# 128-wide attention of a two-layer decoder: another order of scores, transposes and the fourth quarter

## The chip, the cores and the metric

One core of a Trainium2 chip runs the whole program. The metric is the device time in microseconds. A core has engines that run their own instruction lists in order: TensorE (PE in the profile; its weight loads are PEld), VectorE (DVE), ScalarE (ACT), GpSimd (POOL) and the DMA queues of SyncE (SP). They wait for one another by semaphores: a waiting instruction holds up everything behind it on its engine.

## The reference, cut to what matters

The program is a decoder of two layers over `x`, 16 sequences of 64 tokens, 256 wide: attention and cross attention, a mixture of experts, causal attention, then the stage that is changed (a cross attention with 16 heads of width 128), and a second mixture of experts. The changed stage computes, for each sequence `b`:

```python
h  = layernorm(x[b])                                  # 64 x 256
kv = concatenate([ctx[b], h])                         # 128 keys x 256
q  = rope(rms_norm(h @ Wq.T))                         # 16 heads x 64 x 128
k  = rope(rms_norm(kv @ Wk.T))                        # 4 heads x 128 keys x 128
v  = kv @ Wv.T                                        # 4 heads x 128 keys x 128
p  = softmax(q @ k.T / sqrt(128))                     # 4 query heads share a k and a v
x[b] = x[b] + concatenate_heads(p @ v) @ Wo.T
```

## The kernel before, in words

`attention128` works through NT = 8 tiles of 128 tokens, two sequences each. A tile needs:

- `turn_h`: PE transposes the normed input (made by DVE's `norm_a`, POOL's `root` and DVE's `norm_b`); ACT's `h_out` and DVE's `low` split it into two f16 parts.
- `fill(n, u, k)`, k = 0 to 7: six f16 matmuls each (L896), 512 columns of queries (k 0 to 3) or of keys and values of one sequence (4 and 6 keys, 5 and 7 values), into PSUM banks `xpr0` and `xpr1` in turn. A fill waits until the bank's reader is done.
- Each of the six fills of queries and keys is squared by ACT (`square`, L788); then DVE's `rope` sums the squares and makes three products with the tables (L1065 to L1069), and POOL adds the halves (`add`, L733). After the fourth and the sixth `rope`, DVE's `mean_square` and POOL's `rms_root` (L738) make the factors that DVE's `scale` (L1083) applies. Fills 5 and 7 are copied by ACT (`v_copy`).
- `turn_qk(n, i)`: PE transposes a scaled block (L943) into `xpt0` or `xpt1`, ACT copies it out (`qk_out`); i 0 to 3 are queries, 4 and 5 keys ("K4", "K5").
- Four quarters of the attention, each with four heads: `scores` (L905, into `xps0` or `xps1` in turn), DVE's `maxes` (a maximum, L1088, and a small product, L1090), ACT's `exps` (four exponentials, L798), DVE's `normalise` (reciprocal L1095, product L1097), PE's `turn_probs` (L913), ACT's `pt_copy`, PE's `pv` (product with V, L925), ACT's `o_copy` (L808).
- `project`: PE multiplies by Wo in four steps of four matmuls (L933), DVE's `residual` adds to x (L1101).

The tiles are skewed. `skewed` runs `early(0)`, then `mixed(n, n+1)` for n = 0 to 6, and `late(7)`. A `mixed` period does the attention of tile n, the fills, rope and scale of tile n+1, the transposed input of tile n+2, and the projection of tile n-1. Within a period each engine's order is written out by hand, once for each engine; no scheduler changes it. A period begins here, for the reader's counting, with PE's `fill(n+1, 0)`.

The banks `xpt0` and `xpt1` are taken in turn by all transposes of a period, so each transpose has a running number j: it waits until transpose j-2 is copied out, and its reader waits for number j+1. `T_K`, `T_P`, `T_Q`, `T_H` hold these numbers. Eleven transposes are made in a period.

Of the kernel before, what the change touches and what calls it, by code (L numbers as in the profile page):

```python
# [20 lines left out]
NT = B * S // P  # L21
DC = D // P
H = 16
# [642 lines left out]
def attention128(nc, C, w):  # L666
# [5 lines left out]
    with m.stack:  # L672
# [34 lines left out]
        FIRST_T, STEP_T = 6, 11  # L707
        T_K, T_P, T_Q, T_H = (0, 1), (2, 3, 4, 6), (5, 7, 8, 10), 9

        def turns(n, u):  # L710

            base = n * STEP_T + FIRST_T
            if type(n) is int and n == NT - 1:
                base -= 1
                return base, lambda k: (base + k) % 2
            return base, lambda k: (u + k) % 2

        def t_q(n, i):
            return T_Q[i] - (i == 3 and not there(n + 2))
# [42 lines left out]
        def _(act):  # L762
# [15 lines left out]
            def qk_out(j, i, bank):  # L778
# [32 lines left out]
            def early(n, u):  # L811
                h_out(0, 0, 0, 0)
                for k in (0, 1, 2, 3, 4):
                    square(0, k)
                    if k == 1:
                        h_out(1, 1, 1, 1)
                v_copy(0, 0, 5)
                square(0, 6)
                v_copy(0, 0, 7)
                act.wait_ge(t_out, 2)  # L820
                for i in range(4):
                    qk_out(2 + i, i, i % 2)

            def mixed(n, u, n1, u1):
                base, bank = turns(n, u)
                square(n1, 0)
                qk_out(base + T_K[0], 4, bank(T_K[0]))
                square(n1, 1)
                qk_out(base + T_K[1], 5, bank(T_K[1]))
# [12 lines left out]
                exps(n, 3)  # L842
                pt_copy(n, 2, base + T_P[2], bank(T_P[2]))
                qk_out(base + T_Q[0], 0, bank(T_Q[0]))
                v_copy(n1, u1, 7)
                pt_copy(n, 3, base + T_P[3], bank(T_P[3]))
                qk_out(base + T_Q[1], 1, bank(T_Q[1]))
                o_copy(n, u, 2)
                qk_out(base + T_Q[2], 2, bank(T_Q[2]))
                if there(n + 2):  # L850
                    h_out(n + 2, u, base + T_H, bank(T_H))
                o_copy(n, u, 3)
                if there(n + 2):
                    act.wait_ge(t_out, base + T_H + 1)
                qk_out(base + t_q(n, 3), 3, bank(t_q(n, 3)))

            def late(n, u):
                base, bank = turns(n, u)
                qk_out(base, 4, bank(0))
                qk_out(base + 1, 5, bank(1))  # L860
                exps(n, 0)
                exps(n, 1)
                pt_copy(n, 0, base + 2, bank(2))
                pt_copy(n, 1, base + 3, bank(3))
                o_copy(n, u, 0)
                exps(n, 2)
                o_copy(n, u, 1)
                exps(n, 3)
                pt_copy(n, 2, base + 4, bank(4))
                pt_copy(n, 3, base + 5, bank(5))  # L870
                o_copy(n, u, 2)
                o_copy(n, u, 3)
# [4 lines left out]
        def _(pe):  # L877
# [82 lines left out]
            def mixed(n, u, n1, u1):  # L960
                base, bank = turns(n, u)

                def project_before(quarter):
                    if there(n - 1):
                        project(n - 1, 1 - u, quarter)
# [3 lines left out]
                turn_qk(n, 4, base + T_K[0], bank(T_K[0]))  # L969
                project_before(0)  # L970
                fill(n1, u1, 1)
                turn_qk(n, 5, base + T_K[1], bank(T_K[1]))
                project_before(1)
                pe.wait_ge(t_out, base + 2)
# [15 lines left out]
                fill(n1, u1, 6)  # L990
                turn_probs(n, 2, base + T_P[2], bank(T_P[2]))
                turn_qk(n1, 0, base + T_Q[0], bank(T_Q[0]))
                fill(n1, u1, 7)
                turn_probs(n, 3, base + T_P[3], bank(T_P[3]))
                turn_qk(n1, 1, base + T_Q[1], bank(T_Q[1]))
                pv(n, u, 2, base + T_P[2])
                turn_qk(n1, 2, base + T_Q[2], bank(T_Q[2]))
                if there(n + 2):
                    pe.wait_ge(t_out, base + T_H - 1)
                    turn_h(n + 2, u, base + T_H, bank(T_H))  # L1000
                pv(n, u, 3, base + T_P[3])
                turn_qk(n1, 3, base + t_q(n, 3), bank(t_q(n, 3)))

            def late(n, u):
                base, bank = turns(n, u)
                turn_qk(n, 4, base, bank(0))
                turn_qk(n, 5, base + 1, bank(1))
                for quarter in range(4):
                    project(n - 1, 1 - u, quarter)
                pe.wait_ge(t_out, base + 2)  # L1010
                scores(n, 0)
                scores(n, 1)
                turn_probs(n, 0, base + 2, bank(2))
                turn_probs(n, 1, base + 3, bank(3))
                pv(n, u, 0, base + 2)
                scores(n, 2)
                pv(n, u, 1, base + 3)
                scores(n, 3)
                turn_probs(n, 2, base + 4, bank(4))
                turn_probs(n, 3, base + 5, bank(5))  # L1020
                pv(n, u, 2, base + 4)
                pv(n, u, 3, base + 5)
# [6 lines left out]
        def _(dve):  # L1029
# [92 lines left out]
            def mixed(n, u, n1, u1):  # L1122
# [19 lines left out]
                mean_square(n1, 1)  # L1142
                normalise(n, 3)
# [5 lines left out]
                if there(n + 2):  # L1149
                    low(n + 2, u, turns(n, u)[1](T_H))  # L1150

            def late(n, u):
                maxes(n, 0)
                maxes(n, 1)
                residual(n - 1, 1 - u)
                normalise(n, 0)
                normalise(n, 1)
                maxes(n, 2)
# [1061 lines left out]
```

## Time and profile before

| | |
|---|---|
| median of 3 runs | 1053.54 us (1050.61 to 1055.73) |
| profiled execution | 1049.7 us, its span 1047.9 us |
| busy over the span | PE 829.2, DVE 673.1, ACT 486.8, POOL 321.5 us |
| changed stage | from about 453 us to 745 us of the span |
| starts of PE's fill 0 of the periods n = 0 to 6 | 481.90, 513.47, 546.58, 579.66, 612.75, 645.75, 678.70 us |
| last tile's projection starts, its residual ends | 737.49, 745.12 us |

Times are microseconds from the start of the span. In a timeline row stand the start, the length, the engine, the line, the operation, what it writes and reads, its shape, how many were merged, and in brackets how long the engine was idle before it and who ended that idle time.

### The profile page before, as it was taken

Reading aid. Unit: us, or ns where it says so; the run is one execution under the profiler, and the core shown is the slowest. Engines: PE = TensorE matmul, PEld = TensorE weight load, DVE = VectorE, ACT = ScalarE, POOL = GpSimd, SP = SyncE. Lnnn points to the kernel's source line nnn. Section 1 sums busy time; section 2 is a strip of 40 time slices with the busy share of each in tenths; the row PEclk is TensorE's granted clock in tenths of the full one; section 3 lists DMA queues with packets and bytes.
Section 4 is the critical chain, followed back from the end, with each engine's and each line's share of the span. In section 5 each row is a group of like instructions: output and inputs, shape, how many; then the busy total and the mean of one; then the engine's idle time right before and its main releaser. Section 6 shows DMA issues by size and latency. Waiting matters only on the chain. (4 is left out here: it accounts for less than half of the span.)

```text
span 1047.9 us, 16118 instructions
## 1 busy us (share of the span) xinstructions
PE 829.2 (79%) x5470; PEld 545.3 (52%) x5470; DVE 673.1 (64%) x1381; ACT 486.8 (46%) x1235; POOL 321.5 (31%) x281
## 2 busy tenths in 40 slices
PE   3899762347997078767888988897649999999997
PEld 2677642216875066623666766666524444444443
DVE  3778964635764279557788777883346565656654
ACT  1765431115566046514565555654244544454453
POOL 1113763660000554324445424440021221211210
PEclk9999975578999599869999999999659999999999
DMA  9900003227985211000000000000115443444431
GB/s 311 419 29 2 2 2 131 72 80 221 329 301 180 60 48 55 1 1 1 1 1 1 0 0 1 1 1 1 48 50 142 122 123 105 130 115 113 132 91 41
DMA packets 35398, 90.71 MB, mean 87 GB/s; under 512 B 6406, under 2 KB 8969, under 8 KB 34826
## 3 DMA queue, kind: packets, MB, share of 16 engines
q1 hardware_dynamic: 32266, 81.63, 24.4%
q0 software_dynamic: 3072, 8.30, 2.5%
q8 instruction: 35, 0.57, 0.2%
q14 instruction: 25, 0.20, 0.1%
HBM read 67.71 MB, written 22.29 MB: 86 GB/s over the span
## 5 line engine op out<-in xcount | busy, mean ns | idle before, releaser
L1199 POOL TENSOR_TENSOR m1ws<-m1raw,m1ws 128x768 f16<-128x768 f32 x33 | 55.0, 1669 | 219.0 <-ACT m1raw L1202 219.0
L733 POOL TENSOR_TENSOR xqr<-xqr,xt 128x512 f32<-128x512 f32 x48 | 61.2, 1276 | 140.7 <-DVE xt L1069 140.7
L1509 DVE TENSOR_TENSOR m1sg<-m1sg,m1Wb 128x512 f32<-128x512 f32 x66 | 61.1, 926 | 64.0 <-ACT m1sg L1427 53.1
L1469 PE MATMUL m1pg<-m1hs,m1ws 128*128 128x512 f16 x396 | 97.5, 383 | 3.8 <-PEq L58 3.8
L1480 PE MATMUL m1py<-m1ap,m1ws 128*128 128x512 f16 x396 | 96.3, 379 | 1.6 <-DVE m1ap L1521 1.6
L1469 PE MATMUL m1pu<-m1hs,m1ws 128*128 128x512 f16 x396 | 97.0, 381 | 0.0
L1431 ACT ACTIVATE m1ap<-m1ac 128x512 f16<-128x512 f32 x66 | 41.6, 630 | 116.1 <-DVE m1ac L1515 116.1
L1521 DVE TENSOR_TENSOR m1ap<-m1ac,m1ap 128x512 f16<-128x512 f32 x66 | 45.7, 693 | 45.9 <-ACT m1ap L1431 45.9
L1565 POOL DMA_INDIRECT rows<-slots_out,slot x32 | 32.7, 1022 | 116.5 <-DMA slots_out<-m0yo 103.4
L1469 PEld LDWEIGHTS m1pg<-m1hs,m1ws 128*128 128x128 f16 x396 | 38.9, 98 | 51.3 <-issue 5.3
L1480 PEld LDWEIGHTS m1py<-m1ap,m1ws 128*128 128x128 f16 x396 | 38.6, 98 | 48.8 <-DVE m1ap L1521 2.6
L788 ACT ACTIVATE xsq<-xpr 128x512 f32<-128x512 f32 x48 | 28.8, 601 | 75.3 <-PE xpr L896 75.3
L1469 PEld LDWEIGHTS m1pu<-m1hs,m1ws 128*128 128x128 f16 x396 | 39.0, 98 | 47.6 <-issue 1.6
L933 PE MATMUL xpo<-xwo,xOT 128*128 128x256 f32 x256 | 59.6, 380 | 0.7 <-ACT xOT L808 0.7
L798 ACT ACTIVATE xE<-xps,xnb 128x128 f32<-128x128 f32 x128 | 45.5, 379 | 23.5 <-DVE xnb L1090 23.5
L896 PE MATMUL xpr<-xparts,xhs 128*128 128x512 f16 x192 | 49.4, 397 | 8.1 <-DVE xkv L1049 5.2
L1065 DVE TENSOR_REDUCE xss<-xsq 128x4 f32<-128x512 f32 x48 | 32.7, 682 | 35.1 <-ACT xsq L788 34.6
L933 PEld LDWEIGHTS xpo<-xwo,xOT 128*128 128x128 f32 x256 | 47.1, 190 | 7.4 <-ACT xOT L808 1.3
L896 PE MATMUL xpr<-xparts,xkv 128*128 128x512 f16 x192 | 47.6, 387 | 3.4 <-DVE xt L1069 3.4
L1990 PE MATMUL m0ph<-m0xs,m0wg 128*128 128x256 f16 x384 | 48.2, 276 | 2.2 <-DVE m0xs L2026 2.0
L1427 ACT ACTIVATE m1sg<-m1pg 128x512 f32<-128x512 f32 x66 | 39.4, 596 | 18.2 <-PE m1pg L1469 18.2
L1515 DVE SCALAR_TENSOR_TENSOR m1ac<-m1pu,m1sg 128x512 f32<-128x512 f32 x66 | 45.6, 691 | 2.5
(289 smaller groups left out, 1921.5 us busy)
## 6 DMA issues: line engine op xcount, KB each, us to landing
m1Wb<-wt_dram SPq DMA_DIRECT2D x66, 256.0 KB, 4.0
m1raw<-in_m_w SPq DMA_DIRECT2D x33, 384.0 KB, 4.2
slots_in<-zeros SPq DMA_DIRECT2D x1, 8192.0 KB, 26.6
m0rg<-in_m_wgu SPq DMA_DIRECT2D x16, 512.0 KB, 6.9
m0xg<-slots_in SPq DMA_DIRECT2D x32, 256.0 KB, 4.6
slots_out<-m0yo SPq DMA_DIRECT2D x32, 256.0 KB, 3.6
m0rd<-in_m_wd SPq DMA_DIRECT2D x8, 512.0 KB, 7.6
xwo<-in_x_wo SPq DMA_DIRECT2D x1, 2048.0 KB, 17.8
```

The lines of the kernel that those rows point to most:

```text
L733: pool.tensor_tensor(blk, blk, t2[:, k % 2, :, :], ALU.add).then_inc(add_ok, 1)
L798: ins = act.activation(E[:, c, :], p_s[k % 2][:, i, :], ACT.Exp, bias=nb[:, c:c + 1], scale=XSCALE, accum_out=sm[:, c:c + 1])
L896: ins = pe.matmul(p_r[k % 2][:, :, :].rearrange("p h d -> p (h d)"), lhs, rhs, start=(i == 0), stop=(i == 5))
L933: ins = pe.matmul(p_o[u][:, 0:D], OT[:, h, :, :].rearrange("p b q -> p (b q)"), wo[:, h, :], start=(h == 0), stop=(h == XH - 1))
L1199: pool.tensor_tensor(ws[:, u, 1, :], raw[:, u, :], ws[:, u, 0, :], ALU.subtract).then_inc(prep_ok, 1)
L1431: act.activation(ap[:, q, 0, :], ac[:, q, :], ACT.Copy).then_inc(ah_ok, 1)
L1469: ins = pe.matmul(bank[:, :], part(ws, u, sw, c, which), hs[:, sh, c, CH * q:CH * q + CH], start=(k == 0), stop=(k == 5))
L1480: ins = pe.matmul(p_y[c][q][:, :], ws[:, u, sw, GU + P * c:GU + P * c + P], ap[:, q, sa, :], start=(first and k == 0), stop=(last and k == ...
L1509: dve.tensor_tensor(sg[:, q, :], sg[:, q, :], Wb[:, u, CH * q:CH * q + CH], ALU.mult).then_inc(sw_ok, 1)
L1515: dve.scalar_tensor_tensor(ac[:, q, :], p_u[q][:, :], 1.0 / (H_UP * W_UP), sg[:, q, :], ALU.mult, ALU.mult).then_inc(act_ok, 1)
L1521: dve.tensor_tensor(ap[:, q, 1, :], ac[:, q, :], ap[:, q, 0, :], ALU.subtract).then_inc(al_ok, 1)
L1990: ins = pe.matmul(p_h[u][:, which, :], wg[:, u, sw, P * (2 * c + which):P * (2 * c + which) + P], xs[:, u, sx, c, :], start=(i == 0), stop ...
```

## The change

Three things are done in the order of the work; no operation is added or removed, and every shape stays.

1. Scores: PE makes the third quarter's scores right behind fill 4 and the fourth's right behind fill 5, ahead of the transposes and the products with V. DVE takes the third quarter's maxima ahead of `normalise(n, 1)`, the fourth's right behind the fifth `rope`. ACT makes the third quarter's exponentials ahead of the first `pt_copy`, and the fourth's ahead of the second. The two products with V of quarters 1 and 2 stand together, ahead of fill 6.
2. The fourth quarter: `normalise(n, 3)` is DVE's last work of the period. Its transposes, `pt_copy`, product with V and `o_copy` go into the next period, behind its fill 1 ("before" in `ORDER`).
3. The projection of tile n-1 is done in two steps of eight matmuls, before and behind fill 3, instead of four steps of four.

The numbers of the transposes now come from the tuple `ORDER`. `late` is changed in the same manner.

```diff
-        FIRST_T, STEP_T = 6, 11
-        T_K, T_P, T_Q, T_H = (0, 1), (2, 3, 4, 6), (5, 7, 8, 10), 9
+        ORDER = ("K4", "before", "K5", "P0", "P1", "P2", "Q0", "Q1", "Q2", "H", "Q3")
...
 # ScalarE, mixed
+                if there(n - 1):
+                    pt_copy(n - 1, 3, *turn("before"))
+                qk_out(5, *turn("K5"))
+                if there(n - 1):
+                    o_copy(n - 1, 1 - u, 3)
...
                 square(n1, 4)
-                pt_copy(n, 0, base + T_P[0], bank(T_P[0]))
+                exps(n, 2)
+                pt_copy(n, 0, *turn("P0"))
                 v_copy(n1, u1, 5)
-                pt_copy(n, 1, base + T_P[1], bank(T_P[1]))
+                exps(n, 3)
+                pt_copy(n, 1, *turn("P1"))
                 o_copy(n, u, 0)
-                exps(n, 2)
                 o_copy(n, u, 1)
                 square(n1, 6)
-                exps(n, 3)
...
 # TensorE, mixed
                 fill(n1, u1, 1)
+                if there(n - 1):
+                    turn_probs(n - 1, 3, *turn("before"))
+                turn_qk(n, 5, *turn("K5"))
+                if there(n - 1):
+                    pv(n - 1, 1 - u, 3, turn("before")[0])
+                pe.wait_ge(t_out, turn("K5")[0] + 1)
                 scores(n, 0)
                 fill(n1, u1, 2)
                 scores(n, 1)
-                project_before(2)
+                project_before(0, 1)
                 fill(n1, u1, 3)
-                project_before(3)
+                project_before(2, 3)
                 pe.wait_ge(ctx_ok, n1 + 1)
                 fill(n1, u1, 4)
-                turn_probs(n, 0, base + T_P[0], bank(T_P[0]))
+                scores(n, 2)
+                turn_probs(n, 0, *turn("P0"))
                 fill(n1, u1, 5)
-                turn_probs(n, 1, base + T_P[1], bank(T_P[1]))
-                pv(n, u, 0, base + T_P[0])
-                scores(n, 2)
-                pv(n, u, 1, base + T_P[1])
                 scores(n, 3)
+                turn_probs(n, 1, *turn("P1"))
+                pv(n, u, 0, turn("P0")[0])
+                pv(n, u, 1, turn("P1")[0])
                 fill(n1, u1, 6)
...
 # VectorE, mixed
                 rope(n1, 3)
                 mean_square(n1, 0)
+                maxes(n, 2)
                 normalise(n, 1)
                 if there(n - 1):
                     residual(n - 1, 1 - u)
                 rope(n1, 4)
+                maxes(n, 3)
+                normalise(n, 2)
                 if there(n + 2):
                     norm_a(n + 2, u)
-                maxes(n, 2)
                 scale(n1, 0)
-                maxes(n, 3)
-                normalise(n, 2)
                 rope(n1, 5)
                 mean_square(n1, 1)
-                normalise(n, 3)
                 scale(n1, 1)
...
                 if there(n + 2):
-                    low(n + 2, u, turns(n, u)[1](T_H))
+                    low(n + 2, u, turns(n, u)[1]("H")[1])
+                normalise(n, 3)
...
 # TensorE, late
                 turn_qk(n, 4, *turn("K4"))
+                turn_probs(n - 1, 3, *turn("before"))
                 turn_qk(n, 5, *turn("K5"))
+                pv(n - 1, 1 - u, 3, turn("before")[0])
+                pe.wait_ge(t_out, turn("K5")[0] + 1)
+                scores(n, 0)
+                scores(n, 1)
                 for quarter in range(4):
                     project(n - 1, 1 - u, quarter)
```

PE in the period n = 5, from fill 3 to fill 6. `xpr` is the target of a fill, `xpo<-xwo` the projection, `xpt<-ident,xE` the transposed probabilities, `xps` scores, `xpo<-xPT` a product with V. Before:

```order
L896 MATMUL xpr<-xparts,xhs 128x512 x6
L933 MATMUL xpo<-xwo,xOT 128x256 x4
L896 MATMUL xpr<-xparts,xkv 128x512 x6
L913 MATMUL xpt<-ident,xE 128x128 x4
L896 MATMUL xpr<-xparts,xkv 128x512 x6
L913 MATMUL xpt<-ident,xE 128x128 x4
L925 MATMUL xpo<-xPT,xV 128x256 x2
L905 MATMUL xps<-xKT,xQT 128x128 x4
L925 MATMUL xpo<-xPT,xV 128x256 x2
L905 MATMUL xps<-xKT,xQT 128x128 x4
L896 MATMUL xpr<-xparts,xkv 128x512 x6
```

The same place in the changed kernel:

```order
L899 MATMUL xpr<-xparts,xhs 128x512 x6
L936 MATMUL xpo<-xwo,xOT 128x256 x8
L899 MATMUL xpr<-xparts,xkv 128x512 x6
L908 MATMUL xps<-xKT,xQT 128x128 x4
L916 MATMUL xpt<-ident,xE 128x128 x4
L899 MATMUL xpr<-xparts,xkv 128x512 x6
L908 MATMUL xps<-xKT,xQT 128x128 x4
L916 MATMUL xpt<-ident,xE 128x128 x4
L928 MATMUL xpo<-xPT,xV 128x256 x4
L899 MATMUL xpr<-xparts,xkv 128x512 x6
```

Each group of scores now stands ahead of a group of transposes, and both products with V (x4) stand together between the second transposes and fill 6.

DVE in the period n = 5, from the fourth `mean_square` factor to the next `rope`. `xsv` is the mean square, `xE` the normalised probabilities, `x` the residual, `xss` and `xqr` the beginning of a rope, `xmx` and `xnb` a quarter's maxima. Before:

```order
L1076 TENSOR_SCALAR xsv<-xss 128x16
L1095 RECIPROCAL xrc<-xsm 128x4
L1097 TENSOR_TENSOR xE<-xE,xrc 128x512
L1101 TENSOR_TENSOR x<-x,xpo 128x256
L1065 TENSOR_REDUCE xss<-xsq 128x4
L1066 TENSOR_TENSOR xqr<-xpr,xraw 128x512
L1069 TENSOR_TENSOR xt<-xpr,xraw 128x4x64 x2
L1034 BN_STATS xst<-x 128x6
```

The same place in the changed kernel:

```order
L1082 TENSOR_SCALAR xsv<-xss 128x16
L1094 TENSOR_REDUCE xmx<-xps 128x4
L1096 TENSOR_SCALAR xnb<-xmx 128x4
L1101 RECIPROCAL xrc<-xsm 128x4
L1103 TENSOR_TENSOR xE<-xE,xrc 128x512
L1107 TENSOR_TENSOR x<-x,xpo 128x256
L1071 TENSOR_REDUCE xss<-xsq 128x4
L1072 TENSOR_TENSOR xqr<-xpr,xraw 128x512
L1075 TENSOR_TENSOR xt<-xpr,xraw 128x4x64 x2
L1094 TENSOR_REDUCE xmx<-xps 128x4
L1096 TENSOR_SCALAR xnb<-xmx 128x4
```

The third quarter's maxima have come in ahead of the second quarter's normalisation, the residual and the fifth rope; the fourth quarter's follow that rope.

ACT in the same period, between two of its squares (`xsq`). `xPT` is a `pt_copy`, `xV` a `v_copy`, `xOT` an `o_copy`, `xE,xsm` a quarter's four exponentials. Before:

```order
L788 ACTIVATE xsq<-xpr 128x512
L765 ACTIVATE xPT<-xpt 128x512
L792 ACTIVATE xV<-xpr 128x512
L765 ACTIVATE xPT<-xpt 128x512
L808 ACTIVATE xOT<-xpo 128x8x64
L798 ACTIVATE xE,xsm<-xps,xnb 128x128 x4
L808 ACTIVATE xOT<-xpo 128x8x64
L788 ACTIVATE xsq<-xpr 128x512
```

The same place in the changed kernel:

```order
L788 ACTIVATE xsq<-xpr 128x512
L798 ACTIVATE xE,xsm<-xps,xnb 128x128 x4
L765 ACTIVATE xPT<-xpt 128x512
L792 ACTIVATE xV<-xpr 128x512
L798 ACTIVATE xE,xsm<-xps,xnb 128x128 x4
L765 ACTIVATE xPT<-xpt 128x512
L808 ACTIVATE xOT<-xpo 128x8x64 x2
L788 ACTIVATE xsq<-xpr 128x512
```

Each of the two copies of transposed probabilities now has a quarter's exponentials ahead of it.

## Rows read from the trace of the kernel before

**Rows 1.** Busy time by stretch: periods 0, 2 and 6; us, then each engine's busy us.

```profile
481.90:513.47 31.57, 24.81 (x140) 15.82 (x138) 27.51 (x56) 18.82 (x58) 13.97 (x9) 0.97 0.00 1
...
546.58:579.66 33.08, 29.81 (x171) 21.68 (x171) 26.86 (x57) 18.70 (x58) 13.97 (x9) 1.00 0.00 1
...
678.70:711.68 32.98, 30.02 (x173) 21.93 (x173) 25.51 (x50) 18.56 (x56) 12.93 (x8) 1.00 0.00 1
```

**Rows 2.** Timeline of PE in period 2 (starts at 546.58).

```profile
546.58 1.47 PE L896 MATMUL xpr<-xparts,xhs 128*128 128x512 f16 x6 [0.64 <-DVE xkv L1049]
...
547.88 0.60 PE L943 MATMUL xpt<-ident,xqr 128*128 128x128 f32 x4
...
548.32 1.89 PE L933 MATMUL xpo<-xwo,xOT 128*128 128x256 f32 x8
...
550.05 1.46 PE L896 MATMUL xpr<-xparts,xhs 128*128 128x512 f16 x6
...
565.81 1.05 PE L905 MATMUL xps<-xKT,xQT 128*128 128x128 f32 x8
...
566.70 1.03 PE L925 MATMUL xpo<-xPT,xV 128*128 128x256 f32 x4
...
570.96 0.66 PE L913 MATMUL xpt<-ident,xE 128*128 128x128 f32 x4 [1.04 <-DVE xE L1097]
...
574.94 0.65 PE L913 MATMUL xpt<-ident,xE 128*128 128x128 f32 x4 [1.59 <-DVE xE L1097]
...
577.34 0.38 PE L881 MATMUL xpt<-ident,xhn 128*128 128x128 f32 x2
```

**Rows 3.** Timeline of DVE, ACT and POOL in period 2.

```profile
545.69 0.42 DVE L1048 SCALAR_TENSOR_TENSOR xhs<-xpt,xhs 128x256 f16<-128x256 f32 x1 [0.63 <-ACT xkv L775]
...
548.08 0.60 ACT L788 ACTIVATE xsq<-xpr 128x512 f32<-128x512 f32 x1 [0.93 <-PE xpr L896]
...
556.53 0.69 DVE L1065 TENSOR_REDUCE xss<-xsq 128x4 f32<-128x512 f32 x1 [1.03 <-ACT xsq L788]
...
558.39 0.68 DVE L1088 TENSOR_REDUCE xmx<-xps 128x4 f32<-128x512 f32 x1
...
558.55 1.26 POOL L733 TENSOR_TENSOR xqr<-xqr,xt 128x512 f32<-128x512 f32 x1 [3.08 <-DVE xt L1069]
...
559.10 0.73 DVE L1090 TENSOR_SCALAR xnb<-xmx 128x4 f32<-128x4 f32 x1
...
559.75 0.17 DVE L1095 RECIPROCAL xrc<-xsm 128x4 f32<-128x4 f32 x1
...
560.56 0.68 DVE L1065 TENSOR_REDUCE xss<-xsq 128x4 f32<-128x512 f32 x1
...
562.69 1.70 DVE L1097 TENSOR_TENSOR xE<-xE,xrc 128x512 f32<-128x512 f32 x1
...
564.32 0.41 DVE L1101 TENSOR_TENSOR x<-x,xpo 128x256 f32 x1
...
568.46 0.37 ACT L798 ACTIVATE xE<-xps,xnb 128x128 f32<-128x128 f32 x1 [1.85 <-DVE xnb L1090]
...
569.85 0.61 ACT L808 ACTIVATE xOT<-xpo 128x512 f32<-128x512 f32 x1
```

**Rows 4.** Timeline of DVE and POOL at the end of the first tile's ropes.

```profile
477.17 3.56 DVE L1083 TENSOR_TENSOR xqr<-xqr,xsr 128x512 f32<-128x512 f32 x4
...
477.26 1.71 POOL L733 TENSOR_TENSOR xqr<-xqr,xt 128x512 f32<-128x512 f32 x1 [1.74 <-DVE xt L1069]
...
481.07 1.29 DVE L1083 TENSOR_TENSOR xqr<-xqr,xsr 128x512 f32<-128x512 f32 x2 [0.34 <-POOL xsr L738]
```

**Rows 5.** Timeline of PE in the last tile.

```profile
733.31 3.49 PE L925 MATMUL xpo<-xPT,xV 128*128 128x256 f32 x8
...
737.49 7.17 PE L933 MATMUL xpo<-xwo,xOT 128*128 128x256 f32 x32 [0.69 <-ACT xOT L808]
```

**Rows 6.** Stretch of the last tile: us, PE busy us, granted clock, DMA.

```profile
734.00:736.00 2.00, 2.00 (x6) 0.50 0.00 0
```

More of the change, by code:

```diff
@@ L703, in attention128, with turn @@
                  " scaled t_ok t_out s_ok max_ok nb_ok exp_ok rc_ok e_ok o_ok o_out proj_ok x_ok high_ok chigh_ok")
-        FIRST_T, STEP_T = 6, 11
-        T_K, T_P, T_Q, T_H = (0, 1), (2, 3, 4, 6), (5, 7, 8, 10), 9
+        ORDER = ("K4", "before", "K5", "P0", "P1", "P2", "Q0", "Q1", "Q2", "H", "Q3")
         def turns(n, u):
-            base = n * STEP_T + FIRST_T
+            order = [k for k in ORDER if k not in (() if there(n - 1) else ("before",)) + (() if there(n + 2) else ("H",))]
             if type(n) is int and n == NT - 1:
[L714 to L719, printed above, removed]
+                order = order[:6] + ["P3"]
+            base = n * len(ORDER) + (6 if type(n) is int and n == 0 else 4 if type(n) is int and n == NT - 1 else 5)
+            def turn(what):
+                k = order.index(what)
+                return base + k, (base + k if type(n) is int else u + 1 + k) % 2
+            return base, turn
         block = m.stack.enter_context(nc.Block())
@@ L852, in mixed @@
[L852 to L855, printed above, removed]
-            def late(n, u):
-                base, bank = turns(n, u)
-                qk_out(base, 4, bank(0))
-                qk_out(base + 1, 5, bank(1))
+                    h_out(n + 2, u, *turn("H"))
+                    act.wait_ge(t_out, turn("H")[0] + 1)
+                qk_out(3, *turn("Q3"))
+            def late(n, u):
+                _, turn = turns(n, u)
+                qk_out(4, *turn("K4"))
+                pt_copy(n - 1, 3, *turn("before"))
+                qk_out(5, *turn("K5"))
+                o_copy(n - 1, 1 - u, 3)
@@ L960, in mixed, with project_before @@
             def mixed(n, u, n1, u1):
[L961 to L965, printed above, removed]
+                base, turn = turns(n, u)
+                def project_before(*quarters):
+                    for quarter in quarters:
+                        if there(n - 1):
+                            project(n - 1, 1 - u, quarter)
                 pe.wait_ge(t_out, base - 1)
                 fill(n1, u1, 0)
-                turn_qk(n, 4, base + T_K[0], bank(T_K[0]))
-                project_before(0)
+                turn_qk(n, 4, *turn("K4"))
                 fill(n1, u1, 1)
-                turn_qk(n, 5, base + T_K[1], bank(T_K[1]))
-                project_before(1)
-                pe.wait_ge(t_out, base + 2)
+                if there(n - 1):
+                    turn_probs(n - 1, 3, *turn("before"))
+                turn_qk(n, 5, *turn("K5"))
+                if there(n - 1):
+                    pv(n - 1, 1 - u, 3, turn("before")[0])
+                pe.wait_ge(t_out, turn("K5")[0] + 1)
                 scores(n, 0)
@@ L993, in mixed @@
                 fill(n1, u1, 7)
[L994 to L997, printed above, removed]
+                turn_qk(n1, 1, *turn("Q1"))
+                pv(n, u, 2, turn("P2")[0])
+                turn_qk(n1, 2, *turn("Q2"))
                 if there(n + 2):
-                    pe.wait_ge(t_out, base + T_H - 1)
-                    turn_h(n + 2, u, base + T_H, bank(T_H))
@@ L1001, in mixed @@
-                pv(n, u, 3, base + T_P[3])
-                turn_qk(n1, 3, base + t_q(n, 3), bank(t_q(n, 3)))
+                    pe.wait_ge(t_out, turn("H")[0] - 1)
+                    turn_h(n + 2, u, *turn("H"))
+                turn_qk(n1, 3, *turn("Q3"))
             def late(n, u):
-                base, bank = turns(n, u)
-                turn_qk(n, 4, base, bank(0))
-                turn_qk(n, 5, base + 1, bank(1))
+                _, turn = turns(n, u)
+                turn_qk(n, 4, *turn("K4"))
@@ L1014, in late @@
[L1014 to L1015 removed]
                 scores(n, 2)
[L1017 removed]
+                turn_probs(n, 0, *turn("P0"))
                 scores(n, 3)
[L1019 to L1022, printed above, removed]
+                turn_probs(n, 1, *turn("P1"))
+                pv(n, u, 0, turn("P0")[0])
@@ L1023, in late @@
+                turn_probs(n, 2, *turn("P2"))
+                pv(n, u, 1, turn("P1")[0])
+                turn_probs(n, 3, *turn("P3"))
+                pv(n, u, 2, turn("P2")[0])
+                pv(n, u, 3, turn("P3")[0])
                 for quarter in range(4):
```

44 lines of the change are left out of this document (19 added, 25 removed).

## The prediction, as it was put on record

> **What bounds the kernel now.** I read four things in order. First the stretches by period: a steady period takes 33.08 us, PE is busy 29.81 of it, DVE 26.86, ACT 18.70, at a granted clock of 1.00 (the full level, 2.4 GHz) [rows 1]. So PE comes nearest to a bound, and the question is what it waits for in the other 3.3 us. Then PE's timeline: it waits 1.04 us ahead of the third quarter's transposes and 1.59 us ahead of the fourth's, each time for DVE's normalisation, and 0.64 us ahead of the next fill 0, for DVE's low part [rows 2]. The change aims at the first two. Third, the timelines of DVE and ACT, for the length of each step and for what delays it: a product of 128x4 takes 0.73 us at 559.10, because it ends when POOL's addition of 558.55 ends (559.81); a normalisation that falls on such an addition takes 1.70 us [rows 3]. Last, the beginning and the end of the stage, where a scale right behind a rope and a low clock can be seen [rows 4 to 6].
>
> **Price list**, from starts of neighbours. PE: fill 547.88-546.58 = 1.30 to the next instruction, turned block 548.32-547.88 = 0.44, a half of four projection matmuls 550.05-548.32 = 1.73, scores 566.70-565.81 = 0.89, a product with V the same less a little, 0.87 (busy 1.03 against 1.05) [rows 2]. A fill's square starts 548.08-546.58 = 1.50 after the fill and takes 0.60, as any 128x512 copy of ACT does; exponentials 569.85-568.46 = 1.39; rope 558.39-556.53 = 1.86 to the next DVE instruction; normalisation without POOL in the way 560.56-559.75 = 0.81; maxima directly behind a rope 559.10+0.73-558.39 = 1.44, since POOL's addition always starts then; without it 0.90 (0.68, 0.17 and a gap; estimate) [rows 3]. Handing over to another engine costs some 0.04 (fill 0 ends at 548.05, its square starts at 548.08).
>
> **The change, part by part.** Nothing is added or removed, and no DMA is in it, so what counts is one period, walked from its fill 0 (time 0) to the next.
>
> *Start of the period.* Fill 0 at 0, K4 1.30, fill 1 1.74, the fourth quarter's transposes 3.04 (normalised at about 1.0, in the idle time that DVE has ahead of the first rope, so that edit costs DVE nothing), K5 3.48. The product with V must wait for ACT: square 1 at 3.24 to 3.84, then the copy to 4.44, so it starts at 4.45, an idle time of 0.53. Scores 1 at 5.3, fill 2 6.2, scores 2 7.5, eight projection matmuls 8.4, fill 3 11.9, eight more 13.2, fill 4 16.6, third scores 17.9, done at 18.97. The two halves of the projection in one are free.
>
> *The new wait on DVE.* The fourth rope starts at 14.0 as before (560.56-546.58 = 13.98 [rows 3]) and ends at 15.9. Next stand the third maxima, which need the scores of 18.97. Behind them are queued normalisation 1, the residual and the fifth rope. DVE so idles 3.1 us, and goes on: maxima 19.0 to 19.9, normalisation 20.7, residual 21.0 (564.32 to the next rope is 0.33, estimate from its 0.41 busy), fifth rope 21.0 to 22.9. Before, the residual stood at 564.32-546.58 = 17.7 and the rope at 18.1 [rows 3]: 2.9 us late. Normalisation 1 gets out of POOL's way (1.70 to 0.69), which is in these numbers.
>
> *The new wait on PE.* Fourth maxima 22.9 to 24.35 (POOL's fifth addition is in the way), fourth exponentials on ACT 24.4 to 25.75, and only behind these the copy of quarter 2's transposed probabilities, to 26.35. PE's second product with V needs that copy. PE had come to it at 17.92+0.89+0.44+1.30+0.89+0.44+0.87 = 22.8, or 23.1 with the first copy behind the third exponentials. So PE stands still for 3.3 us, with fills 6 and 7 and three blocks behind it. This is the dear one. Then product 26.4, fill 6 27.3 (before: 21.9, one scores' 0.89 behind 567.57 = 566.70+0.87), its square 28.8 to 29.4, sixth rope 29.4 to 31.3.
>
> *The end of the period.* The wait for normalisation 3 is gone, but block Q1 needs scale 1, which needs the sixth rope: Q1 at 31.3+0.07+0.75 = 32.1. Behind a rope the early tile shows what follows: the scale goes first and POOL's addition is stretched to 1.71, and scale 4 starts 481.07-477.17 = 3.90 after the first scale, the last two take 1.29 [rows 4]. So the last scale ends at 31.3+0.07+3.90+1.29 = 36.5, the low part follows, and the next fill 0 starts 546.58-545.69 = 0.89 after the low part's start [rows 2, 3], at 37.35. The way over the transposed input is shorter: with Q2 at 34.2 behind the delayed third scale, `turn_h` at 34.6 and 579.66-577.34 = 2.32 more [rows 2] make 37.0.
>
> A steady period is thus 37.3 against 33.08: **+4.3**. Bounds: with no POOL in the way of the fourth maxima 0.55 less; and if the low part does not wait for the last scale 0.35 less, so +3.3 at least; upward, the first scale at the contended 1.70 instead of 0.70 adds up to 1.0, so +5.3 at most. I take the middle, because rows 3 and 4 show just these neighbours.
>
> The Trainium skill says in "SBUF — State Buffer", section "Who interferes with whom", that a VectorE instruction with two SBUF inputs and a GpSimd one that reads SBUF shut each other out for the whole instruction, whoever starts first. The 1.70 against 0.69 agrees. By it alone a scale just behind the rope could also lose the port; that is the upper bound.
>
> *Sum.* Period 0 (31.57 now [rows 1]) has no tile before it, so no projection stands ahead of its fill 4 and DVE hardly waits for the third scores; only the stop ahead of the second product with V remains, and the same walk gives +1.9. Periods 1 to 5: 5 x 4.26 = 21.3. Period 6 and the last tile together: the sixth rope again at +29.4; K4 after scale 4; normalisation 3 is no longer hidden, its transposes come at 37.5, scores at 39.7; the projection of tile 6 (16 matmuls, 6.9 us) now covers the first two quarters' exponentials; the remaining chain of maxima, exponentials and copies ends with the last copy at 58.0. Before, that was 737.49-678.70 = 58.8, in which the two last products took 3.49 instead of 1.74 at a granted clock of 0.50 [rows 5, 6]. So -0.8. Together +22.4 us.
>
> **The clock.** In the last tile, after a stretch in which PE stopped again and again for normalisations, the granted clock fell to 0.50 (the 1.2 GHz level), and the low stretch cost 3.49-1.74 = 1.75 us [rows 5, 6]. In the changed kernel each period has a complete stop of 3.3 us, longer than any in a steady period now, and some 2 us at its end. If the clock falls after the first, fill 6 on the chain runs slow; what it can cost is between 0 and 1.75, I take 1.1, for six periods: +6.6, or 7 with some at the end. The Trainium skill, "TensorE: Matmul & The Clock Gate", section "HAM oscillation — how this bites in real kernels", tells of the same thing, a loop whose every burst starts cold behind a wait. It speaks against this change; by the rows alone the fall is likely, not sure.
>
> So the profiled execution of 1049.7 would become 1049.7+22.4+7 = 1079; the median of the runs, 3.8 above that execution, becomes 1053.5+29 = **1082 us**.
>
> **The rivals.**
>
> - *Waits as walked, clock stays up.* 1053.5+22.4 = 1076. For it: a gap on PE alone did not always bring the clock down (at 1.00 in all steady periods, with waits of 1.59). Chance 0.27; forecast with the clock 0.50.
> - *The clock falls twice in most periods*, at the stop and again at the period's end, so that fill 0 to scores start slow: 2 x 1.75 x 6 = 21 on top of 22.4, at most 1097. 0.11.
> - *The other side: the removed waits decide.* If the order on ACT let the copy pass in time, the period would be PE's work plus the way over `turn_h`: fill 0 to `turn_h` 28.8, and 2.32, so 31.1, 1.95 less than now, over six periods 12 us: 1042. It decides if the fourth maxima were ready before 19.6 or so. Against it: these wait for the fifth rope, which waits for fill 4 at 16.6. 0.07.
> - *The moved waits cancel*: the stop on PE takes 1.0 us instead of 3.3, because DVE's order costs less than read. Then each period is as before. 0.05, 1053.
>
> Half a per cent, 5.3 us, is what measuring can tell from no change. Slower by more: 0.50+0.27+0.11 = 0.88; within: 0.05; faster: 0.07. The range from 1066 to 1095 leaves out about two in ten: the other side, the cancelled case, and the far end of the twice fallen clock. Its lower end is +3.3 a period for five periods less 4 for the ends of the stage (1053.5+12.5), its upper end the clock cost near its maximum in most periods.
>
> **What would show it.** In the trace of the changed kernel: starts of fill 0 about 37 to 39 us apart; PE idle about 3 us ahead of the product with V behind the second transposes, released by ACT's copy; DVE idle about 3 us ahead of the third maxima, released by scores; no wait of PE for the third or fourth normalisation; granted clock under 1.00 in the steady periods; the last tile shorter by about 5 us from its K4. I am wrong if the period is under 34 us, if the stop on PE is under 1.5 us, or if the fifth rope starts before the third maxima.

## The result, and the profile after

The changed kernel takes 1087.96 us in the median of 4 runs (1083.94 to 1089.87), the kernel before 1054.63 us in 4 runs (the three told above and one more of 1057.54). The ratio is 1.0319, 95% interval 1.0292 to 1.0346. The profiled execution took 1087.24 us with a span of 1085.4 us, 37.5 more than the span before. That is more than the 33.3 between the medians, because the profiled execution of the kernel before (1049.7 us) was shorter than any of its four runs.

The busy times by stretch, with the columns of [rows 1], of periods 0, 2, 4 and 6:

```profile
482.19:515.42 33.23, 24.22 (x131) 15.33 (x130) 25.66 (x54) 17.88 (x56) 13.49 (x9) 0.94 0.00 0
...
554.67:593.32 38.65, 32.18 (x171) 22.50 (x171) 26.25 (x57) 18.87 (x58) 13.60 (x9) 0.96 0.00 1
...
632.56:673.35 40.79, 35.20 (x170) 24.28 (x171) 26.21 (x57) 19.18 (x57) 13.62 (x9) 0.87 0.00 0
...
713.36:751.00 37.64, 32.92 (x168) 23.13 (x168) 23.36 (x49) 18.48 (x55) 12.96 (x8) 0.91 0.00 1
```

A steady period takes 38.65 to 40.79 us (fill 0 of periods 1 to 6 starts at 515.42, 554.67, 593.32, 632.56, 673.35 and 713.36) against 33.08. DVE and ACT are busy for about as long as before; PE's busy time in a steady period has grown from 29.81 to between 32.18 and 35.20 us without one added instruction, and the granted clock is 0.87 to 0.96 in place of 1.00.

PE's timeline of period 2 of the changed kernel, whose fill 0 starts at 554.67 (compare [rows 2]):

```profile
554.67 1.47 PE L899 MATMUL xpr<-xparts,xhs 128*128 128x512 f16 x6 [0.90 <-DVE xkv L1055]
...
559.04 1.13 PE L928 MATMUL xpo<-xPT,xV 128*128 128x256 f32 x4 [0.30 <-ACT xPT L765]
...
572.59 1.05 PE L908 MATMUL xps<-xKT,xQT 128*128 128x128 f32 x8
...
576.75 1.13 PE L928 MATMUL xpo<-xPT,xV 128*128 128x256 f32 x4
...
581.02 1.71 PE L928 MATMUL xpo<-xPT,xV 128*128 128x256 f32 x4 [3.15 <-ACT xPT L765]
...
582.52 2.61 PE L899 MATMUL xpr<-xparts,xkv 128*128 128x512 f16 x6
...
588.54 0.65 PE L946 MATMUL xpt<-ident,xqr 128*128 128x128 f32 x4 [1.25 <-DVE xqr L1089]
```

The waits for normalisations are gone. In their place PE stops for 3.15 us ahead of the second product with V, released by ACT's copy. The six matmuls of the fill behind it then take 2.61 us instead of 1.46. At the end PE waits again, for block Q1 (1.25) and for the low part (0.90).

DVE, ACT and POOL in the same period (compare [rows 3]):

```profile
573.68 0.69 DVE L1094 TENSOR_REDUCE xmx<-xps 128x4 f32<-128x512 f32 x1 [2.98 <-PE xps L908]
...
575.30 0.41 DVE L1107 TENSOR_TENSOR x<-x,xpo 128x256 f32 x1
...
575.63 0.68 DVE L1071 TENSOR_REDUCE xss<-xsq 128x4 f32<-128x512 f32 x1
...
577.48 0.68 DVE L1094 TENSOR_REDUCE xmx<-xps 128x4 f32<-128x512 f32 x1
...
577.64 1.26 POOL L733 TENSOR_TENSOR xqr<-xqr,xt 128x512 f32<-128x512 f32 x1 [2.82 <-DVE xt L1075]
...
578.20 0.73 DVE L1096 TENSOR_SCALAR xnb<-xmx 128x4 f32<-128x4 f32 x1
...
578.96 0.37 ACT L798 ACTIVATE xE<-xps,xnb 128x128 f32<-128x128 f32 x1 [1.86 <-DVE xnb L1096]
...
580.36 0.61 ACT L765 ACTIVATE xPT<-xpt 128x512 f32<-128x512 f32 x1
...
585.80 0.69 DVE L1071 TENSOR_REDUCE xss<-xsq 128x4 f32<-128x512 f32 x1 [4.58 <-ACT xsq L788]
...
587.73 0.69 DVE L1089 TENSOR_TENSOR xqr<-xqr,xsr 128x512 f32<-128x512 f32 x1
...
587.82 1.72 POOL L733 TENSOR_TENSOR xqr<-xqr,xt 128x512 f32<-128x512 f32 x1 [6.18 <-DVE xt L1075]
...
588.33 1.36 DVE L1048 TENSOR_SCALAR xhn<-x,xmv 128x256 f32 x1
```

To be read from top to bottom: DVE waits 2.98 us for the third scores, with normalisation, residual and fifth rope (575.63) behind; the fourth maxima follow that rope, and their small product takes 0.73 us beside POOL's addition; only then come the exponentials (578.96) and the copy (580.36) that lets PE go on. The sixth rope starts at 585.80, 31.1 us after fill 0, after 4.58 us without work for DVE. Behind it POOL's addition is stretched to 1.72 and DVE's norm_b to 1.36.

PE's busy time and granted clock in steps of 2 us over the stop:

```profile
578.00:580.00 2.00, 0.00 (x0) 1.00 0.00 0
...
580.00:582.00 2.00, 0.98 (x3) 0.86 0.00 0
...
582.00:584.00 2.00, 2.00 (x6) 0.50 0.00 0
...
584.00:586.00 2.00, 2.00 (x13) 0.79 0.00 0
```

The clock falls to 0.50 with the stop: in period 2 half a microsecond behind its end, in others up to 1.3 us ahead of it (in period 1 at about 540.5 us, with PE going on at 541.84). It does so in each of the seven periods, and twice more with fill 0, behind the waits at the period's end (632 to 636 and 673 to 677 us). The last tile's products with V and the start of the last projection (compare [rows 5]):

```profile
771.04 1.98 PE L928 MATMUL xpo<-xPT,xV 128*128 128x256 f32 x8
...
773.71 7.17 PE L936 MATMUL xpo<-xwo,xOT 128*128 128x256 f32 x32 [0.69 <-ACT xOT L808]
```

The eight matmuls took 1.98 us, at the full clock, against 3.49 at 0.50 in the kernel before. From the last tile's first transposed block (K4, 751.59 us here, about 710.7 before) to this projection pass 22.1 us instead of 26.8.

### The profile page after: what moved, and what is told of

Read it like the earlier page. It is cut to its first block and busy times, and to the rows that moved or that the text cites. A ratio compares the mean times of both kernels' runs of the same rounds, so it can differ in the third digit from the quotient of the medians.

```text
span 1085.4 us, 16122 instructions
## 1 busy us (share of the span) xinstructions
PE 852.6 (79%) x5470; PEld 557.1 (51%) x5470; DVE 665.0 (61%) x1381; ACT 489.7 (45%) x1235; POOL 319.0 (29%) x281
## 5 line engine op out<-in xcount | busy, mean ns | idle before, releaser
L733 POOL TENSOR_TENSOR xqr<-xqr,xt 128x512 f32<-128x512 f32 x48 | 64.4, 1341 | 175.6 <-DVE xt L1075 175.6
L1571 POOL DMA_INDIRECT rows<-slots_out,slot x32 | 32.7, 1023 | 111.7 <-DMA slots_out<-m0yo 98.7
L928 PE MATMUL xpo<-xPT,xV 128*128 128x256 f32 x128 | 41.2, 452 | 25.0 <-ACT xPT L765 24.8
L899 PE MATMUL xpr<-xparts,xhs 128*128 128x512 f16 x192 | 53.3, 420 | 9.2 <-DVE xkv L1055 6.8
L899 PE MATMUL xpr<-xparts,xkv 128*128 128x512 f16 x192 | 54.4, 427 | 3.3 <-DVE xt L1075 3.3
```

What stands on the lines that cost most here:

```text
L733: pool.tensor_tensor(blk, blk, t2[:, k % 2, :, :], ALU.add).then_inc(add_ok, 1)
L899: ins = pe.matmul(p_r[k % 2][:, :, :].rearrange("p h d -> p (h d)"), lhs, rhs, start=(i == 0), stop=(i == 5))
L928: ins = pe.matmul(p_o[(u + k) % 2][:, 256 * g:256 * g + 256], V[:, u, k // 2, 2 * (k % 2) + g, :], PT[:, k % 2, 2 * g:2 * g + 2, :].rearra ...
```

## The experiments

Eight kernels were run. The change as a whole stands at 1.0319. Each ratio is to the kernel before in the same chip's runs; periods are means over periods 1 to 5 of the one profile of each kernel, from the starts of fill 0; "end" is from fill 0 of period 6 to the last residual's end.

| kernel | ratio, 95% interval | period | end |
|---|---|---|---|
| before | 1 | 33.05 | 66.42 |
| changed | 1.0319, 1.0292 to 1.0346 | 39.59 | 67.98 |
| e1_copy_first | 1.0063, 1.0046 to 1.0081 | 35.15 | 63.62 |
| e2_spare_matmuls | 1.0220, 1.0187 to 1.0252 | 36.96 | 67.00 |
| e3_quarter4_alone | 0.9965, 0.9945 to 0.9986 | 33.25 | 62.04 |
| e4_scores_alone | 1.0316, 1.0278 to 1.0354 | 38.00 | 71.79 |
| e5_square_first | 0.9982, 0.9965 to 1.0000 | 34.30 | 62.38 |
| e6_norm_first | 1.0248, 1.0225 to 1.0271 | 37.58 | 66.30 |
| e7_input_early | 0.9859, 0.9837 to 0.9881 | 31.55 | 63.29 |
| e8_input_early_before | 1.0038, 1.0018 to 1.0058 | 34.01 | 66.43 |

**e1_copy_first**, from the changed kernel, ACT in `mixed`:

```diff
                 v_copy(n1, u1, 5)
-                exps(n, 3)
                 pt_copy(n, 1, *turn("P1"))
+                exps(n, 3)
                 o_copy(n, u, 0)
```

> One pair on ScalarE is exchanged in the mixed periods of the changed kernel: the copy of the second quarter's transposed probabilities stands ahead of the fourth quarter's exponentials. Theory A (the stop ahead of the second product with V comes from this copy being queued behind exponentials that wait for the fifth rope): PE's stop of 3.15 us ahead of that product falls under 0.5 us; but the exponentials now sit ahead of the square of fill 6, so the sixth rope comes only about 1.8 us earlier (27.6 instead of 29.4 after fill 0) and not 3.2. With the clock falling less often, the period goes from 39.6 to 35.5 to 37 us, the kernel from 1088 to about 1066 to 1074. Rival B (the period is set by VectorE's late third maxima and the long end behind the sixth rope, the stop on PE is only slack): the period changes by less than 0.5 us, the kernel stays within 3 us of 1088.

Measured: one exchanged pair takes away 2.6 of the 3.2 per cent. In period 2 (fill 0 at 544.26) the two products with V run without a stop, and the sixth rope starts 27.3 us after fill 0 (31.1 in the changed kernel):

```profile
566.32 2.03 PE L928 MATMUL xpo<-xPT,xV 128*128 128x256 f32 x8
...
571.56 0.69 DVE L1071 TENSOR_REDUCE xss<-xsq 128x4 f32<-128x512 f32 x1 [0.74 <-ACT xsq L788]
```

The period is 34.8 us where the clock stays up and 36.4 in the one period (613.97 to 650.38) in which it fell at fill 0. A ratio of 1.0063 is 1061 us beside the 1054.63 of before, 5 less than the lower end of what was expected. The period is below the 35.5 to 37 expected, and the clock fell in only one of the five. Rival B is out: the stop is no slack.

**e2_spare_matmuls**, from the changed kernel, PE in `mixed`; `spare` waits for the residual and issues twelve f16 matmuls of 128x512 into the bank that the next product overwrites:

```diff
                 pv(n, u, 0, turn("P0")[0])
+                spare(n, u, u1)
                 pv(n, u, 1, turn("P1")[0])
```

> The changed kernel with 12 spare matmuls (128x512, f16, 0.22 us each at the full level, 2.6 us together) on PE ahead of the second product with V, written into the PSUM bank that this product overwrites; they fill the stop of 3.2 us and change no result. Theory A (some 2.2 us of each period's +6.5 are the granted clock that falls after the stop): the clock stays at 1.00 there, the period falls from 39.6 to about 37.5, where the walk over the waits alone puts it, and the kernel from 1088 to about 1075. Rival B (the low clock is only a sign of idleness and costs nothing on the chain of waits): the period stays at 39.6 or grows by what the spare matmuls add, the kernel is 1088 or more.

Measured: with 77 more matmuls in the record (84 were added) the kernel is a per cent faster than the changed one. In period 2 (fill 0 at 545.62) the stop is 0.57 us, since the spare work fills it, but the next product starts no sooner in the chain of waits, 26.35 us after fill 0 as in the changed kernel; the fill behind it takes 1.46 us, and the clock of the whole period is 1.00:

```profile
568.64 2.75 PE L935 MATMUL xpo<-xparts,xhs 128*128 128x512 f16 x12
...
571.97 1.13 PE L928 MATMUL xpo<-xPT,xV 128*128 128x256 f32 x4 [0.57 <-ACT xPT L765]
...
572.94 1.46 PE L899 MATMUL xpr<-xparts,xkv 128*128 128x512 f16 x6
...
545.62:582.58 36.96, 33.08 (x182) 23.05 (x183) 26.27 (x57) 18.80 (x58) 13.60 (x9) 1.00 0.00 1
```

The period is 36.96 at a granted clock of 1.00, against 39.59: the clock costs 2.6 us a period, where 2.2 were expected. Rival B is out.

**e3_quarter4_alone**, from the changed kernel: scores, maxima and exponentials of quarters 3 and 4 back where they were in the `mixed` periods; the last tile keeps the changed order.

```diff
 # TensorE, mixed
                 fill(n1, u1, 4)
-                scores(n, 2)
                 turn_probs(n, 0, *turn("P0"))
                 fill(n1, u1, 5)
-                scores(n, 3)
                 turn_probs(n, 1, *turn("P1"))
                 pv(n, u, 0, turn("P0")[0])
+                scores(n, 2)
                 pv(n, u, 1, turn("P1")[0])
+                scores(n, 3)
 # ScalarE and VectorE: exps(n, 2), exps(n, 3), maxes(n, 2), maxes(n, 3), normalise(n, 2) likewise
```

> One part alone: the fourth quarter's normalisation, transposes and product with V in the next period and the projection in two steps, as in the changed kernel, but scores, maxima and exponentials of quarters 3 and 4 in the order of the kernel before. Theory A (the order of scores and exponentials brings the stop; moving quarter 4 by itself costs little): no stop above 1 us on PE, clock at 1.00, the fifth rope at about 18.7 after fill 0; but 1.3 us of quarter 4's work and 0.5 us of waiting stand ahead of fill 6, so the period is about 34 us against 33.1, the kernel about 1054.6 + 6 x 0.9 - 3 (shorter last tile) = 1057. Rival B (moving quarter 4 is what lengthens the period, since everything behind fill 1 comes later): 1075 or more. Rival C (the two removed waits pay): 1042 to 1048.

Measured: 0.9965, so this part of the change is a small gain. The period is 33.25 us, hardly longer than before, not the 34 expected; the gain comes from the end, 62.04 against 66.42 us, of which about 1.5 us are the low clock in the kernel before's last products with V (3.49 against 1.98 us). PE does what it did in [rows 1] and the clock stays up:

```profile
549.13:582.39 33.26, 30.19 (x171) 21.84 (x171) 26.89 (x57) 18.73 (x58) 13.55 (x9) 1.00 0.00 1
```

**e4_scores_alone**, from the kernel before: the same groups moved forward, quarter 4 and the last tile left alone.

```diff
 # TensorE, mixed (order of the changed kernel)
+                scores(n, 2)
                 turn_probs(n, 0, base + T_P[0], bank(T_P[0]))
                 fill(n1, u1, 5)
+                scores(n, 3)
                 turn_probs(n, 1, base + T_P[1], bank(T_P[1]))
                 pv(n, u, 0, base + T_P[0])
-                scores(n, 2)
                 pv(n, u, 1, base + T_P[1])
-                scores(n, 3)
 # ScalarE and VectorE likewise
```

> The other part alone: the kernel before, with scores, maxima and exponentials of quarters 3 and 4 moved forward as in the changed kernel; quarter 4 stays in its period, the projection in four steps, the last tile as before. Theory A (this order makes the stop): PE stops for about 3.6 us ahead of the second product with V, the clock falls in most periods, the period is 36.2 us from the waits alone and 37.5 to 39 with the clock, the kernel 1054.6 + 6 x 3.1 = 1073 without and 1080 to 1090 with the clock. Rival B (it is the combination with quarter 4 that stops PE): period under 34, the kernel within 5 us of 1055.

Measured: 1.0316, all of the loss. In period 2 (fill 0 at 552.72) stands the same stop:

```profile
577.20 2.07 PE L925 MATMUL xpo<-xPT,xV 128*128 128x256 f32 x4 [3.15 <-ACT xPT L765]
...
579.06 2.10 PE L896 MATMUL xpr<-xparts,xkv 128*128 128x512 f16 x6
```

Its profiled period of 38.0 lies in the expected 37.5 to 39, the ratio in the upper half of what was expected. Rival B is out. The periods are shorter than in the changed kernel (38.0 against 39.59) and the end, with the old last tile, longer (71.79 against 67.98).

One period of this run prices the clock without any spare work. In period 3 (fill 0 at 591.48) the stop is the same, but the clock stays at 1.00:

```profile
615.96 1.13 PE L925 MATMUL xpo<-xPT,xV 128*128 128x256 f32 x4 [3.15 <-ACT xPT L765]
...
591.48:627.73 36.25, 29.96 (x171) 21.80 (x171) 26.25 (x57) 18.90 (x59) 13.55 (x9) 1.00 0.00 0
```

It takes 36.25 us, where 36.2 were expected from the waits alone; the other four take 37.95 to 38.76 (in two of them the clock falls twice). So the waits cost 3.2 us here and the clock 1.7 to 2.5 more, and a stop of 3.15 us does not bring the clock down every time.

**e5_square_first**, from the changed kernel:

```diff
                 v_copy(n1, u1, 5)
-                exps(n, 3)
                 pt_copy(n, 1, *turn("P1"))
                 o_copy(n, u, 0)
                 o_copy(n, u, 1)
                 square(n1, 6)
+                exps(n, 3)
```

> The changed kernel with ScalarE's fourth exponentials put behind the square of fill 6 (behind the copy of quarter 2's probabilities and both output copies too). e1_copy_first took the stop off PE, and its period is 34.8 us; there the square of fill 6 still stands behind the exponentials, which wait for the fourth maxima. Theory A (what sets the period is when the sixth rope starts, and that needs this square): the sixth rope starts some 1.4 us sooner, the period is 33.4 to 33.8 us, the clock stays at 1.00, ratio to the kernel before 0.995 to 1.000. Rival B (after e1 the late fifth rope is the bound): period and ratio as in e1, 34.8 us and 1.006.

Measured: 0.9982. The sixth rope starts 572.50-546.02 = 26.5 us after fill 0, 0.8 sooner than in e1 instead of 1.4, and the period is 33.9 us where the clock stays up (35.7 in the one where it fell), a little over the 33.4 to 33.8 expected. So with ACT's list fitted to it the changed kernel is back at the time of the kernel before. The order of scores is not free by that: e3, which has the rest of the change, has a period of 33.25 us, 0.7 less.

**e6_norm_first**, from the changed kernel, DVE:

```diff
-                maxes(n, 2)
                 normalise(n, 1)
                 if there(n - 1):
                     residual(n - 1, 1 - u)
+                maxes(n, 2)
                 rope(n1, 4)
```

> The changed kernel with VectorE's third maxima behind the second normalisation and the residual instead of ahead of them; all else as in the changed kernel, the stop on PE too. Theory A (VectorE's wait of 3.0 us for the third scores delays the two steps behind it, and by them the fifth rope, the fourth maxima and all that follows): VectorE does these two steps inside the wait, the fifth rope starts about 1.1 us sooner, the period falls by 1.1 us, and the clock falls as before; ratio 1.024 to 1.028 against 1.032. Rival B (that wait is slack): ratio unchanged at 1.03 or more.

Measured: 1.0248 against 1.0319. DVE's wait for the third scores is 0.83 us and the stop on PE 2.12 us, a microsecond less, in period 2 (fill 0 at 555.00):

```profile
574.00 0.69 DVE L1094 TENSOR_REDUCE xmx<-xps 128x4 f32<-128x512 f32 x1 [0.83 <-PE xps L908]
...
580.30 1.91 PE L928 MATMUL xpo<-xPT,xV 128*128 128x256 f32 x4 [2.12 <-ACT xPT L765]
...
582.01 2.40 PE L899 MATMUL xpr<-xparts,xkv 128*128 128x512 f16 x6
```

The mean period is 2.0 us shorter, not 1.1. Period 2, in which the clock falls once in both kernels, is 1.04 shorter (37.61 against 38.65). The clock still falls with the stop (2.40 us for the fill), but at no period's end, and it comes back sooner (in period 1 after 3.4 us at 0.50, in the changed kernel after 6.8). The remainder is put down to that; no run shows it by itself.

**e7_input_early**, from e3_quarter4_alone:

```diff
-        ORDER = (..., "P2", "Q0", "Q1", "Q2", "H", "Q3")
+        ORDER = (..., "P2", "Q0", "H", "Q1", "Q2", "Q3")
 # ScalarE
                 qk_out(0, *turn("Q0"))
+                h_out(n + 2, u, *turn("H"))
                 v_copy(n1, u1, 7)
+                act.wait_ge(t_out, turn("H")[0] + 1)
                 qk_out(1, *turn("Q1"))
 # TensorE: fill 0 waits for base - 3 instead of base - 1, and
                 fill(n1, u1, 7)
+                turn_h(n + 2, u, *turn("H"))
                 turn_qk(n1, 1, *turn("Q1"))
 # VectorE
                 scale(n1, 0)
+                norm_b(n + 2, u)
                 maxes(n, 3)
...
                 scale(n1, 1)
-                norm_b(n + 2, u)
+                low(n + 2, u, ...)
                 scale(n1, 2)
                 scale(n1, 3)
+                low_ctx(n + 2, u)
                 scale(n1, 4)
                 scale(n1, 5)
-                low(n + 2, u, ...)
                 normalise(n, 3)
```

> A version meant to beat both. From e3_quarter4_alone, with one more change: the transposed input of tile n+2 is made earlier. norm_b goes ahead of the fourth maxima, turn_h behind fill 7 and ahead of block Q1, h_out ahead of the copy of values, the low part of it directly behind scale 1, the low part of the context behind scale 3; PE's fill 0 no longer waits for the last block's copies. Theory (in e3 the end of the period, from the sixth rope to the next fill 0, is 7.5 us long because the low part waits for the last scales, which wait for POOL's root): fill 0 starts when PE is through with Q3, about 31.5 us after the last fill 0 instead of 33.25, six times: 10 us less than e3, ratio to the kernel before about 0.986. Rival B (VectorE is the bound by then, with POOL's addition in its way): period 33 us or more, ratio 0.995 to 1.00.

Measured: 0.9859, the fastest of all, 1037.14 us against 1052.63 beside it. A steady period is 31.55 us and PE is busy 30.10 of it:

```profile
545.63:577.29 31.66, 30.10 (x173) 21.88 (x170) 25.98 (x57) 18.84 (x58) 13.48 (x9) 1.00 0.00 1
```

Before fill 0 PE waits no more; its largest wait is 0.56 us, for the third quarter's normalisation. Rival B is out.

**e8_input_early_before**, the same edit in the kernel before (quarter 4's transposes and copies stay, `normalise(n, 3)` ahead of `scale(n1, 1)`):

> The kernel before with only the early transposed input of e7_input_early; quarter 4 stays in its own period, with its normalisation ahead of scale 1. Theory A (both moves are needed: with the normalisation of quarter 4 in POOL's way ahead of scale 1 and its transposes ahead of block Q1, the end of the period is still long): the wait of 0.64 us ahead of fill 0 goes and little else, the period is about 32.2 us against 33.08, ratio 0.994 to 0.997. Rival B (the early input alone gives all of e7's gain): period 31.6 us, ratio 0.986 to 0.989. Rival C (no gain, the wait moves ahead of block Q1): ratio 0.999 to 1.001.

Measured: 1.0038, slower; none of the three was right. Period 2 (fill 0 at 546.91) shows why:

```profile
573.75 1.26 POOL L733 TENSOR_TENSOR xqr<-xqr,xt 128x512 f32<-128x512 f32 x1 [3.99 <-DVE xt L1071]
...
573.87 1.70 DVE L1099 TENSOR_TENSOR xE<-xE,xrc 128x512 f32<-128x512 f32 x1
...
575.70 0.65 PE L912 MATMUL xpt<-ident,xE 128*128 128x128 f32 x4 [1.43 <-DVE xE L1099]
...
576.18 0.38 PE L880 MATMUL xpt<-ident,xhn 128*128 128x128 f32 x2
...
577.56 0.42 DVE L1047 SCALAR_TENSOR_TENSOR xhs<-xpt,xhs 128x256 f16<-128x256 f32 x1 [1.40 <-ACT xkv L775]
...
579.05 0.65 PE L942 MATMUL xpt<-ident,xqr 128*128 128x128 f32 x4 [0.49 <-ACT xQT L765]
```

Quarter 4's normalisation still runs into POOL's addition (1.70) and PE waits for it ahead of the transposes; the transposed input stands behind them, so the low part, now ahead of scales 2 to 5, comes when DVE has waited 1.40 us; ACT's copy of block Q1 must wait for it, and PE's block Q2 (579.05) for that copy. In e7 quarter 4 stands in neither place. The early input pays only with quarter 4 out of the way.

## Why the prediction was right

Forecast were +29 us on the median; measured are 1087.96-1054.63 = +33.3. In the profiled executions the stage grew by 36.0 us, where the forecast's terms make 29.4, so the forecast was nearer on the median than in the stage: the waits were nearly as forecast, the clock over twice as dear. By its steps:

**The wait on DVE.** Predicted 3.1 us ahead of the third maxima, released by the scores; measured 2.98. That it delays what follows is shown by e6, which takes most of it away and shortens period 2 by 1.04 us.

**The stop on PE.** Predicted 3.3 us ahead of the second product with V, starting again 26.4 us after fill 0; measured 3.15 us, and 581.02-554.67 = 26.35. That it comes from the order on ACT, behind exponentials that wait for the fifth rope, is shown by e1, and that it belongs to the order of scores, not to quarter 4, by e3 and e4.

**The end of the period.** Predicted: the first scale keeps the port, POOL's addition is stretched to 1.71, the last scales wait for the root. The addition took 1.72 and the scale 0.69. The root took 1.69 instead of 2.10 us beside another neighbour, so the end is about 0.4 shorter than walked: the walk gave 37.3, and e2, in which the clock stays up, has 36.96. DVE's norm_b, which came second, took 1.36 instead of 0.40. The rule of the Trainium skill in "SBUF — State Buffer", section "Who interferes with whom", fits: who starts first has the port for the whole instruction. The way over the transposed input, forecast at 37.0, came second by only some 0.2 us: in period 2 ACT's copy of it ends at 592.26 us, and DVE's low part starts at 592.44, directly behind the last scale.

**The ends of the stage.** Period 0: +1.9 predicted for the waits alone, 33.23-31.57 = +1.7 measured, in which the price of the clock's fall at the stop is contained; the kernel before began this period with 2 us of low clock (to about 484.0), the changed one with 0.3. So this hit is partly luck. Period 6 with the last tile: -0.8 predicted, 67.98-66.42 = +1.6 measured. There the clock fell after the stop of period 6, for which the forecast had 0.4; with the stop taken away (e1, e3) the end is 63.6 and 62.0, so the gain in the last tile (4.7 us from its K4, "about 5" predicted) is real and was paid back. In e2, which fills the stop, the end is 67.0: its clock fell to 0.50 for some 3 us from 731.3 us on, in the last tile.

**The clock.** The term that was clearly mis-sized. Predicted 1.1 us a period, 7 in all; measured 39.59-36.96 = 2.6 us a period. It fell with the stop in all seven periods, and the low level lasted not for fill 6 alone: in period 2 the product with V took 1.71 instead of 1.13 and the fill 2.61 instead of 1.46, together 1.7 on the chain (38.65-36.96); in period 3 the low level reached the transposes behind them too (1.06 and 0.99 instead of 0.60), and the period is 2.2 us longer than in e2. So one fall can cost more than the 1.75 taken as its upper bound. That figure was itself misread: the eight products of [rows 5] take 1.98 us at the full clock, not 1.74, so that fall had cost 3.49-1.98 = 1.51 us on them. Twice it fell again at fill 0, and those two periods are the longest (40.79 and 40.01). Of the steady periods only one (38.65 us) lies within the 37 to 39 us named as the sign to look for; the other four lie above. The rival with two falls in most periods gave 1097; it happened in two of seven.

The sum in spans: +1.7, 5 x 6.54 = +32.7 and +1.6 make 36.0 of the 37.5; the rest lies outside these periods. Of the 32.7, about 19.6 are the waits (5 x (36.96-33.05), 21.3 predicted) and 13.1 the clock.

The two removed waits, 1.04 and 1.59 us, are gone as intended and bought nothing here. e3 tells why: there the fourth quarter's wait is gone and the third's down to 0.50 us, but PE meets its next limit, the way from the sixth rope to the low part, within the same period, and waits 0.90 us ahead of fill 0 instead of 0.64.

## What to carry to other kernels

When an order is written out for each engine, moving work forward on one of them is only as good as the lists of the others: here PE had its scores early, but ACT put their exponentials ahead of a copy that PE needed sooner, and one exchanged pair of lines was worth 2.6 per cent. Walk the new period from one instruction to the next with the durations of the old trace; a queue in which a short, urgent step stands behind a step that waits for another engine is what to look for. A stop of PE of some three microseconds can cost the clock besides: here it fell at each of seven stops, which put 2.6 us a period on top of the 3.9 of the waits (in e4 one period of five escaped), and a wait that is removed shows its worth only when the next one is removed with it (e3 and e8 against e7).

## What the runs showed of the hardware that was not expected

- A shorter stop was enough to bring the granted clock to 0.50, and the longer one did not always do it: the 2.1 us stops of e6 did so in all five steady periods, the 3.15 us stops of e4 in four of five. In the kernel before, waits of 1.59 us never did in a steady period.
- Twelve spare matmuls a period, whose results nobody reads, made the kernel 1 per cent faster, because the granted clock stayed at 1.00 over the wait (e2 1.0220 against 1.0319).
- POOL's power over 128x8 took 2.09 us in the kernel before and 1.69 us in the changed one; what is beside it on DVE differs (before: the end of a normalisation, a scale, norm_b and the next scale; changed: the end of norm_b and two scales). Why is open.
